# A gated graph network on one core: graph product with a stationary split adjacency, turned out of PSUM, three groups staggered by slots

## The reference

```python
y = einsum('nm,bmd->bnd', adj, x); x = layernorm(x + y @ weight + bias)      # first layer
h = x
for _ in range(3):                                                            # three gated steps
    a = einsum('nm,bmd->bnd', adj, h);  av = concat([a, a])
    z = sigmoid(lin(av, w3) + lin(h, u3));  r = sigmoid(lin(av, w4) + lin(h, u3))
    hv = tanh(lin(av, w5) + lin(r * h, u5))
    h = (1 - z) * h + z * hv
out = layernorm(x + h)
```

## Time and profile before

| | |
|---|---|
| median of three runs | 1674.75 us (1674.03 to 1675.79) |
| the profiled execution, its span | 1671.51 us, 1669.7 us |
| PE busy | 1643.2 us (98%), 8608 matmul records |
| DVE busy | 1364.2 us (82%) |
| ACT busy | 836.8 us (50%) |
| POOL busy | 162.4 us (10%) |
| transfers | 166.48 MB, 100 GB/s over the span |
| chain that ended last | PE 91%, DVE 4%, the rest 5% |
| TensorE clock granted, mean | 0.994 |

### The profile page before, as it was taken

The page is one execution under the profiler, slowest core; times in us unless marked ns, Lnnn a source line. Parts: engine busy times, 40 slices in busy tenths (PEclk is TensorE's granted clock), DMA queues, the critical chain, the costliest instruction groups (busy, mean ns, idle before and its releaser), DMA issues.

```text
span 1669.7 us, 24669 instructions
## 1 busy us (share of the span) xinstructions
PE 1643.2 (98%) x8608; PEld 1410.7 (84%) x8608; DVE 1364.2 (82%) x2217; ACT 836.8 (50%) x1190; POOL 162.4 (10%) x168
## 2 busy tenths in 40 slices
PE   6999999999999999999999999999999999999997
PEld 6888888888888888888888888888888888888885
DVE  5678888888888888888888878888888888888777
ACT  3445454554545454545445454545455455545553
POOL 3001001010100101001010010100101010010000
PEclk8999999999999999999999999999999999999998
DMA  3123242232422333224232332424224232243221
GB/s 112 51 76 126 82 125 83 88 126 96 123 87 83 126 109 105 88 88 136 90 118 83 99 115 88 126 82 125 84 86 126 98 125 86 82 128 110 91 75 63
DMA packets 172021, 166.48 MB, mean 100 GB/s; under 512 B 16352, under 2 KB 147936, under 8 KB 172000
## 3 DMA queue, kind: packets, MB, share of 16 engines
q1 hardware_dynamic: 172000, 166.20, 31.2%
HBM read 84.35 MB, written 81.79 MB: 100 GB/s over the span
## 4 chain that ended last, share of the span: by engine, by line
PE 91%; DVE 4%; SPq 1%; DMA 1%; issue 1%; ACT 1%; DVEq 0%
PE ps_r L307 44%; PE ps_h L307 29%; PE ps_x L317 10%; PE ps_z L350 5%; PE ps_z L317 3%; DVE hv L678 1%; SPq L220 1%; DVE hv L674 1%; DMA h_moved_in<-h_scratch 1%; DVE h_blocks L687 1%; DMA x_in_b<-x 0%; DVE h_t_a L680 0%; ACT hv L499 0%; DVE w_lo L577 0%; ACT h_nat L463 0%
## 5 line engine op out<-in xcount | busy, mean ns | idle before, releaser
L558 ACT ACTIVATE z_sb<-ps_r,bias_z 128x512 f32<-128x512 f32 x192 | 129.9, 686 | 96.9 <-PE ps_r L307 96.7
L499 ACT ACTIVATE hv<-ps_h,bias_h 128x512 f32<-128x512 f32 x192 | 132.3, 689 | 86.2 <-PE ps_h L307 85.9
L674 DVE TENSOR_TENSOR hv<-hv,h_t_a 128x512 f32<-128x512 f32 x96 | 78.3, 815 | 118.9 <-ACT hv L499 118.9
L535 ACT ACTIVATE rh<-ps_r,bias_r 128x512 f32<-128x512 f32 x192 | 126.6, 684 | 91.9 <-PE ps_r L307 90.9
L678 DVE TENSOR_TENSOR hv<-hv,z_sb 128x512 f32<-128x512 f32 x192 | 160.7, 837 | 7.8
L577 DVE TENSOR_TENSOR rh_lo<-rh,rh_hi 128x512 fp32r<-128x512 f32 x192 | 128.4, 689 | 9.4
L463 ACT ACTIVATE rh_hi<-rh 128x512 fp32r<-128x512 f32 x192 | 119.6, 630 | 28.5 <-DVE rh L762 28.5
L317 PEld LDWEIGHTS ps_x<-adjt,h_nat 128*128 128x128 f32 x1024 | 123.4, 191 | 8.7 <-ACT h_nat L463 4.3
L307 PE MATMUL ps_h<-rh_hi,u_hi 128*128 128x512 f32 x384 | 127.1, 412 | 0.0
L317 PE MATMUL ps_x<-adjt,h_nat 128*128 128x128 f32 x1024 | 125.3, 275 | 1.2 <-ACT h_nat L463 1.2
L307 PE MATMUL ps_r<-a_hi_b,w_hi 128*128 128x512 f32 x384 | 121.3, 397 | 0.0
(11 more groups left out here) (141 smaller groups left out, 3749.2 us busy)
## 6 DMA issues: line engine op xcount, KB each, us to landing
h_scratch<-h_blocks SPq DMA_DIRECT2D x128, 256.0 KB, 2.0
h_moved_in<-h_scratch SPq DMA_DIRECT2D x512, 64.0 KB, 2.0
h_scratch<-h_blocks SPq DMA_DIRECT2D x30, 512.0 KB, 2.6
x_in_a<-x SPq DMA_DIRECT2D x16, 512.0 KB, 4.7
x_in_b<-x SPq DMA_DIRECT2D x16, 512.0 KB, 5.7
out<-result_a SPq DMA_DIRECT2D x16, 512.0 KB, 3.0
h_moved_in_a<-h_scratch SPq DMA_DIRECT2D x60, 128.0 KB, 3.5
h_moved_in_b<-h_scratch SPq DMA_DIRECT2D x60, 128.0 KB, 3.0
```

The source lines that it names most:

```text
L499: act.activation(hv[:, c, :], ps_h[:, c, :], ACT.Tanh, bias=bias_h[:, c:c + 1]).then_inc(hv_ready, 1)
L535: r = act.activation(rh[:, c, :], ps_r[:, c, :], ACT.Sigmoid, bias=bias_r[:, c:c + 1])
L558: z = act.activation(z_sb[:, c, :], ps_r[:, c, :], ACT.Sigmoid, bias=bias_z[:, c:c + 1])
L674: dve.tensor_tensor(hv[:, c, :], hv[:, c, :], before[:, c, :], ALU.subtract).then_inc(diff_ready, 1)
```

## The change

The hardware loop and the pairs are gone. The program is written out slot by slot: step t of group g is in slot 3g + 4t, so that each slot has one step and three groups are under way. A new group starts every third slot, and the next step of a group comes four slots later. There are 96 steps, in slots 0 to 101; the slots 1, 2, 5, 96, 99 and 100 have no step, since no group is at that point at the start or at the end. The engines walk over slots from -6; slots -6 to -1 hold the first groups' first layer.

The graph product is made the other way round. The split adjacency is stationary and the split `h` (nodes on the partitions, 512 columns) moves past it: six matmuls in place of eight float32 ones. So `h` in the nodes' layout has to be split (`node_high` on ScalarE, `node_low` on VectorE), and the result has the nodes on the partitions. VectorE turns it in blocks of 32x32 straight out of PSUM (`graph_blocks`), SP moves it through DRAM (`write_a`, `read_a`), and ScalarE and VectorE split what has landed. All three steps move `h` now. The state's update is made in one piece of 1024 columns. Both normalisations go from VectorE to ScalarE, the residual is added in the nodes' layout, and GpSimd works out the shift (two more small operations a norm).

The new parts and the order in which PE, VectorE, ScalarE and SP take them (cut to the core):

```diff
-            def graph(psum, nat, signal):
-                for c in range(C):
-                    for b in range(G):
-                        mm = pe.matmul(psum[:, c, b * N:(b + 1) * N], nat[:, b, c * P:(c + 1) * P], adjt[:, :],
-                                       start=True, stop=True)
+            def graph(s):
+                pe.wait_ge(nat_hi_ready, n + 1)
+                if n >= 1:
+                    pe.wait_ge(a_blocks_ready, n)
+                for c in range(C):
+                    for k, (w, v) in enumerate(((adj_hi, nat_hi), (adj_lo, nat_hi), (adj_hi, nat_lo))):
+                        if c == 0 and k == 2:
+                            pe.wait_ge(nat_lo_ready, n + 1)
+                        mm = pe.matmul(ps_a[:, c, :], w[:, :], v[:, c, :], start=k == 0, stop=k == 2, ...)
+            # PE
+            for s in range(BEGIN, END + 1):
+                if s + 1 in nth: graph(s + 1)
+                if s in nth: state_product(s)                                  # u3
+                if (g := group_at(s, GRAPH)) is not None: first_graph(g)       # waits y_added of g - 1
+                if (g := group_at(s, WEIGHTS)) is not None: first_weights(g)
+                if s in nth: gates(s)                                          # w4, w5, w3, u5
+            # VectorE
+            for s in range(BEGIN, END + 5):
+                if s + 1 in nth: graph_blocks(s + 1)
+                if s - 1 in nth: update(s - 1); state_blocks(s - 1)
+                if s + 2 in nth: node_low(s + 2)
+                if s in nth: reset(s)                                          # r*h and its lo part
+                if s + 1 in nth: state_low(s + 1); graph_low(s + 1)
+                ...                       # first_graph_low, first_sum, first_blocks, residual
+            # ScalarE
+                if s - 1 in nth: candidate(s - 1, 1)
+                if s + 2 in nth: node_high(s + 2)
+                if s + 1 in nth: state_high(s + 1)
+                ...                       # first_graph_high
+                if s in nth: reset_gate(s); reset_high(s)
+                if s + 1 in nth: graph_high(s + 1)
+                ...                       # first_norm, result_norm
+                if s in nth: update_gate(s); candidate(s, 0)
+            # SP
+                if h0_next is not None: write_h0(h0_next)
+                if s + 1 in nth: write_a(s + 1)
+                if h0_next is not None: read_h0(h0_next)
+                if s + 1 in nth: read_a(s + 1)
+                ...                       # store, load
+                if s - 1 in nth: move_h(s - 1)
```

More of the change, by code:

```diff
@@ L36 @@
 C = 2
+Q = 32
+BLOCKS = P // Q
 STEPS = 3
-SLOTS = 2 * STEPS
 EPS = 1e-5
@@ L296, in _ @@
+            for g in range(2):
+                sp.wait_ge(out_stored[g], 16 * (GROUPS // 2))
         @block.tensor
@@ new lines, in gates, with a_parts @@
+            def gates(s):
+                n, half = nth[s], nth[s] % 2
+                def a_parts(k, c):
+                    if (k, c) == (0, 0):
+                        pe.wait_ge(a_hi_ready, n + 1)
+                    if (k, c) == (2, 0):
+                        pe.wait_ge(a_lo_ready, n + 1)
+                if n == 0:
+                    pe.wait_ge(gates_ready, 2)
+                split_product(ps_r, "w4", a_hi[half], a_lo[half], False, True, r_done, a_parts)
+                if n >= 1:
+                    pe.wait_ge(hv_ready, 2 * n)
+                else:
@@ L445, in slot @@
-                split_product(ps_h, "u5", rh_hi, rh_lo, False, True, h_done, None, range(1, C))
-            def pair(p, first, last):
-                for k in range(SLOTS):
-                    slot(p, k, first, last)
-            run_pairs(pe, pair)
-            def last_state_there(c):
-                pe.wait_ge(last_h_ready, 2 * PAIRS - 1 + c + 1)
-            to_nodes(ps_z, h_t[1], last_t_done, last_state_there)
+                    pe.wait_ge(r_ready, 2 * n + o + 1)
+                    split_product(ps_r, "w3", a_hi[half], a_lo[half], False, True, z_done, None, range(o, o + 1))
@@ L566, in pair @@
-            def pair(p, first, last):
-                for k in range(SLOTS):
-                    slot(p, k, first, last)
-            run_pairs(act, pair)
+            copy(adj_hi[:, :], adjt[:, :]).then_inc(adj_hi_ready, 1)
+            for s in range(BEGIN, END + 5):
+                if s - 1 in nth:
+                    candidate(s - 1, 1)
+                if s + 2 in nth:
+                    node_high(s + 2)
+                if s + 1 in nth:
+                    state_high(s + 1)
+                if (g := group_at(s, GRAPH)) is not None:
+                    first_graph_high(g)
+                if s == BEGIN + 1:
+                    act.wait_ge(gate_sum, 4)
+                    for name in NAMES:
+                        copy(gate_hi[name][:, :, :], gate_raw[name]).then_inc(gates_hi_ready, 1)
+                if s in nth:
+                    if nth[s] == 0:
+                        act.wait_ge(biases_ready, 1)
+                    reset_gate(s)
+                    reset_high(s)
+                if s + 1 in nth:
+                    graph_high(s + 1)
+                if (g := group_at(s, NORM)) is not None:
+                    first_norm(g)
+                if (g := group_at(s, RESULT)) is not None:
+                    result_norm(g)
+                if s in nth:
+                    update_gate(s)
+                    candidate(s, 0)
@@ new lines, in graph_low, with reset @@
+            def graph_low(s):
+                n, half = nth[s], nth[s] % 2
+                dve.wait_ge(a_hi_ready, n + 1)
+                low_part(in_quadrants(a_lo[half]), chunks_first(a_landed[half]),
+                         in_quadrants(a_hi[half])).then_inc(a_lo_ready, 1)
+            def reset(s):
+                n, (g, t) = nth[s], at(s)
+                for c in range(C):
+                    dve.wait_ge(r_ready, 2 * n + c + 1)
+                    dve.tensor_tensor(in_quadrants(rh)[:, c], in_quadrants(rh)[:, c], h_t[g % H_RING][:, :, c, :],
+                                      ALU.mult).then_inc(rh_ready, 1)
+                for c in range(C):
+                    dve.wait_ge(rh_hi_ready, 2 * n + c + 1)
+                    low_part(rh_lo[:, c, :], rh[:, c, :], rh_hi[:, c, :]).then_inc(rh_lo_ready, 1)
@@ L800, in pair @@
-            def pair(p, first, last):
-                for k in range(SLOTS):
-                    slot(p, k, first, last)
-            run_pairs(dve, pair)
-            end = slot_no(PAIRS - 1, SLOTS - 1)
-            dve.tensor_tensor(h0_t[1][:, :, :], h0_t[1][:, :, :], h_t[1][:, :, :], ALU.add).then_inc(last_sum_ready, 1)
-            dve.wait_ge(last_t_done, 1)
-            row_statistics(out_norm, rows_of(ps_x_nat), out_stats)
-            dve.wait_ge(out_stats, 2 * PAIRS - 1)
-            mean_and_variance(out_norm, out_var)
@@ L863, in pair @@
[L863 to L876 removed]
+                pool.wait_ge(rstd_ready, g + 1)
```

925 lines of the change are left out of this document (400 added, 525 removed).

## The result

| | before | changed |
|---|---|---|
| median, lowest to highest | 1674.39 us (1671.73 to 1675.79) | 1697.16 us (1695.48 to 1698.56) |
| profiled execution, its span | 1671.51, 1669.7 | 1698.56, 1696.7 |
| PE busy, share of the span | 1643.2, 98% | 1614.2, 95% |
| DVE / ACT / POOL busy | 82% / 50% / 10% | 85% / 56% / 15% |
| transfers | 166.48 MB | 272.45 MB |

The changed kernel is slower: ratio 1.0138, 95% interval 1.012 to 1.0155. The forecast was 1691.5 (1665 to 1730), so the direction and the range held and its most likely value was 5.7 too low. PE does 29 us less work and still ends 27 us later: it idles 56 us more.

What follows compares the result with a forecast made beforehand. The prediction took PE's sum of matmuls as the bound. Savings of 42.2, 1.0 and 4.3 us against costs of 10.7, 20, 24 and 9.5 gave +16.7, so 1691.5 us from a median of 1674.75, range 1665 to 1730.

Steps and rivals of the forecast that it cites:

- graph product: On PE in each of 96 steps: six matmuls take 1.36 us in place of 1.80, saving 42.2 us.
- turn on PE, small waits: On PE: one group's turn back to nodes goes, about 1.0 us, and small waits of 4.3 us go.
- start to the first `w4`, less 1.8: At the start: w4 begins at 48.4 instead of 35.9, with one graph product already done; 10.7 us lost.
- empty slots, start: Slots 1, 2 and 5: PE idles 12.7 and some 6 us, plus half clock; 20 us lost.
- empty slots, end: Slots 96, 99 and 100: PE waits 7.8 and 14.3 us, plus half clock; 24 us lost.
- tail: After the last matmul: 23.3 us instead of 13.6, counted as 9.5 more allowing for overlap.
- With one stretch at half clock: Empty slots at the start: one half-clock stretch of PE, added to idle times of 12.7 and some 6, gives 20 us.
- the static order couples groups that have nothing to do with each other: Empty slots: PE's next work waits behind other groups' updates and movements in the engines' order; 20 us at the start.
- (1): Start, empty slots and tail: edges mostly hidden, costing about 35 us, so the saving of 47.5 wins: 1662 us; chance 0.24.
- (2): Middle: VectorE becomes the bound if turns out of PSUM cost twice: 1745 us, or 1705 to 1715 at half that; chance 0.14.
- (3): Movements through DRAM take 10 us in place of 7 under load, 1.1 a group and 21 at edges: 1745 us; chance 0.08.
- (4): Graph product on PE isn't cheaper, say 0.27 us a matmul: saving 17, time 1717 us; chance 0.03.

Runs made afterwards that it cites:

- sum first: Changed kernel with VectorE doing the first layer's sum and statistics of groups 1 and 2 before `a`'s low part, in slots -1 and 2: 1690.68 us.
- old product in slot 101: Changed kernel with the earlier kernel's graph product (float32 `h` stationary, no turn or movement of `a`) in the last slot alone: 1686.38 us.
- turned on PE: Changed kernel with the earlier graph product in slots 0, 98, 101, first-layer sums ahead of `a`'s low part, last state turned by TensorE: 1669.75 us.
- The two lengths: Both kernels at full length and with half as many groups; at half, the changed kernel took 903.70 us and the one before 858.39 us.
- the run with the low part first: Changed kernel with VectorE forming `nat_lo` before the update of the slot before, in slots 1, 5, 96 and 99: 1701.02 us.
- the run with more passes: Changed kernel with one more VectorE pass of 128x1024 in each of the 95 later slots, into an unread buffer: 1734.03 us.
- the last run: The kernel of "turned on PE", with slot 3 also on the earlier graph product and its step run before slot 4's product: 1665.68 us.

## Why the prediction was right, and where it was off

The forecast was the right case of the five. Term by term, on the spans; what the runs add stands in the last column:

| term | forecast | by the two traces | shown by |
|---|---|---|---|
| graph product | -42.2 | -42.2 | 50.90 against 49.58 a group |
| turn on PE, small waits | -5.3 | -5.0 | slots 7 to 95 in 1460.15 us |
| start to the first `w4`, less 1.8 | +10.7 | +12.3 | sum first: -6 there |
| empty slots, start | +20 | +24.6 | slot 3's step moved: -4.1 by the medians |
| empty slots, end | +24 | +27.2 | old product in slot 101: -11.6 |
| tail | +9.5 | +9.8 | turned on PE: -7.4 |

The middle was right to 0.3 us, because it was a sum of PE's starts and nothing hid in it. The edges came to 73.9 us by the traces where I had 64.2, 9.7 too little; 0.3 more is the middle, and 0.3 rounding. (The two lengths give 67.6 as the fixed part. Of the 6.3 between the two numbers 3.9 are medians against profiled executions; the rest is the turn on PE, which comes once, and such small waits of the kernel before as its rate of 50.99 doesn't hold.) The median is off by 5.7 only, and that is luck: the profiled execution of before had lain 3.2 below its median, and that of after lies 1.4 above.

**The step that was too small is the one on the clock: "With one stretch at half clock" at the start, "With two stretches at half clock, less a little for quiet transfers" at the end.** The forecast's waits are 12.7 + 6 at the start and 7.8 + 14.3 at the end; what its 20 and 24 have beyond that is the clock. In the trace the two are told apart like this: at full clock one start of PE follows the other after 0.227 us (512 columns), 0.121 (256) or 0.1125 (the float32 blocks of 128). What the distance of two starts has more than that counts as wait if PE was idle between them, and as lower clock if it wasn't.

| empty slots | forecast: waits, clock | traced: waits, clock |
|---|---|---|
| start | 18.7, 1.3 | 17.7, 6.8 |
| end | 22.1, 1.9 | 19.5, 7.7 |

So the waits were forecast 1.0 and 2.6 too long, and what follows them 5.5 and 5.8 too short; the two errors partly cancel. At the start there are three longer stretches at half clock, from 49.99, 69.47 and 121.71, of 2.7, 3.8 and 6.1 us; at the end four, of 5.7, 3.2, 3.2 and 2.7. Each costs half its length. By the same count over the whole of PE's work from 30 us on, the run with the low part first has waits of 44.5 where the changed kernel has 44.0, and 20.8 of lower clock for 18.5: what it won came back as other waits. Its loss is of the size of the added lower clock; how long such a stretch lasts also differs from execution to execution, as the last section shows.

**A smaller miss is "a movement is 2.62 from write to the first read, 1.3 to the fourth, 3.0 to its landing: 7 us".** It is so for a movement alone (6.8 to 6.9 us from the write to the first operation on what landed, in the tail and for the first `h`). The first `a` had a load issued ahead of it and took 8.6, which is the +1.6 of the start to the first `w4`. The last `a` took 8.0, and the shorter waits above have that in them.

**The step that was right in number but not in its reading** is "the static order couples groups that have nothing to do with each other". For the first layer's sums that was so, and moving them gave 7.5. For the waits on `nat_lo` it was only half so. The forecast names the update as what stands ahead of them, but that update is the next link of the same kind of chain; the run with the low part first paid back all it won. I had the chains' lengths nearly right and the remedy wrong, which the forecast itself didn't need.

**The rivals.** (1) Hidden edges would have needed less than 47.5; they were 68 to 74. Its argument, that movements may take less than 7 us, fails: 6.8 to 6.9 alone, 8.0 and 8.6 beside others. Nor did PE run ahead at a wait: from 64.52 to 69.47 it stands at `nat_lo`, with the first layer's weight product behind it, whose operands VectorE had finished at 58.8. (2) VectorE as the bound: the turn costs 0.69, from PSUM as from SBUF, and VectorE was 92% busy rather than 94. The run with more passes shows that the rival wasn't far: about 2.2 us a group. By the Trainium skill (VectorE: DVE Perf Modes, the section on the TRN2 errata) the PSUM source would have had 65 ns more; 691 against 700 ns doesn't show them. (3) Longer movements under load: they did get longer. In the middle a state's movement takes 8.6 us in the median, from its write's issue to the landing of its last read, and up to 12.5, the longest right behind a load of `x`. That of `a` takes 7.2, and in the 28 slots with `h0` ahead of it 9.1; the 10 that the rival asked for it reaches in two of them. PE waited for none, so the mechanism is there and stays hidden. The Trainium skill (DMA: Bandwidth & Descriptors, Latency and other measured facts) has HBM access rise from 0.2 to 2 us at high load; the 2.6 us of a write alone against 4.2 beside another is in that direction, though no run here separates HBM from the queue. (4) A dearer product: a matmul of it takes 0.227, so this rival is out.

**What stays open.** How much of a longer movement is the queue's order, and how much the shared engines, wasn't tried: all go through SP. The price of the lower clock at the edges is counted from traces alone; no run changed the clock and left the waits. By that count the last run has 29.1 of waits and 10.1 of lower clock, for 44.0 and 18.5 in the changed kernel.

## What to carry to other kernels

A schedule that is finer pays its filling and draining once and its gain per round: run both versions at half the length, and two subtractions give rate and fixed part, which no single profile does. At the edges, follow one group's chain through all engines before you reorder; a wait can be removed only where what you delay isn't on the chain itself, and the best remedies were a shorter way for the last unit (11.6 and 7.4 us) and real work put into the wait. Price a wait of TensorE together with what follows it: here 37.2 us of waits in the empty slots brought 14.5 of lower clock. And here a VectorE at 97% busy was already the bound.
